# A block factorisation on one core: two units applied ahead instead of one, and part of the i·U halves made by a VectorE shuffle

## The reference, cut to what matters

```python
def cal_wfft_ortho(weight, n, cout, cin):
    vfft = jnp.fft.rfft2(weight, s=(n, n), norm='ortho')      # n = 34
    vfft = jnp.transpose(vfft, (2, 3, 0, 1))
    vH = jnp.conj(jnp.swapaxes(vfft, -1, -2))
    wfft = vH @ vfft                                          # 127 x 127 complex, per frequency
    ...
    wfft = wfft + eps[..., None, None] * jnp.eye(m)
    ortho = I - 2.0 * (vfft @ jnp.linalg.solve(wfft, vH))
xfft = rfft2(pad(groupnorm(x)));  zfft = ortho @ xfft
return x + irfft2(zfft)[crop] + bias
```

## Time and profile before

| | |
|---|---|
| median of three runs | 2853.52 us (2851.91 to 2857.53) |
| span of the profiled execution | 2851.4 us |
| outside the span, against the median | 2.1 us |
| PE / weight load / DVE busy | 2466.2 / 2018.1 / 1900.5 us |
| ACT / POOL busy | 1390.0 / 503.3 us |
| mean granted clock of PE | 0.928 |

### The profile page before, as it was taken

How to read it: one execution, slowest core, us unless ns; L and a number is a source line. 1 busy time by engine, 2 the same in 40 slices (tenths; PEclk the granted TensorE clock), 3 DMA queues, 4 the chain that set the end, 5 groups by cost and what they waited for, 6 DMA issues and landing times. The chain is left out here.

```text
span 2851.4 us, 89547 instructions
## 1 busy us (share of the span) xinstructions
PE 2466.2 (86%) x37953; PEld 2018.1 (71%) x37953; DVE 1900.5 (67%) x4779; ACT 1390.0 (49%) x3469; POOL 503.3 (18%) x872
## 2 busy tenths in 40 slices
PE   4975977999999899998987978787888888997999
PEld 4954744666566687777866767675776776987998
DVE  6852446888979768585768888897886885002444
ACT  1422422344353466665764646464565563772332
POOL 0002412121310011111111101010322221440000
PEclk7977988999999999999998989898899999997999
DMA  5274476331411283663835334361312323555874
GB/s 193 90 127 85 77 144 157 113 122 68 154 45 44 37 165 77 120 121 70 170 62 102 74 77 96 56 122 31 112 61 61 113 69 115 165 164 125 213 215 138
DMA packets 562604, 310.03 MB, mean 109 GB/s; under 512 B 484616, under 2 KB 495496, under 8 KB 561368
## 3 DMA queue, kind: packets, MB, share of 16 engines
q1 hardware_dynamic: 520896, 183.58, 30.7%
q0 software_dynamic: 41312, 120.73, 13.1%
HBM read 162.85 MB, written 141.30 MB: 107 GB/s over the span
## 5 line engine op out<-in xcount | busy, mean ns | idle before, releaser
L1499 DVE SCALAR_TENSOR_TENSOR arena<-arena,psum 128x512 f32<-128x512 f32 (+2 forms) x608 | 399.0, 720 | 322.5 <-PE psum L1063 322.4
L1063 PE MATMUL psum<-arena 32*128 32x128 f32 (+1 forms) x9280 | 300.4, 274 | 13.7 <-ACT arena L1250 9.7
L1040 PEld LDWEIGHTS psum<-arena 32*32 32x32 f32 x9280 | 162.0, 137 | 202.6 <-issue 201.1
L1063 PEld LDWEIGHTS psum<-arena 32*128 32x128 f32 x9280 | 279.0, 186 | 35.1 <-ACT arena L1250 20.3
L1002 PE MATMUL psum<-arena 128*32 128x256 f32 (+1 forms) x3696 | 262.7, 379 | 35.0 <-DMA arena<-plain 27.9
L1211 ACT COPY arena<-arena 32x128 f32<-32x128 f32 (+2 forms) x608 | 244.6, 402 | 92.4 <-DVE arena L1510 71.9
L1446 DVE TENSOR_TENSOR arena<-arena 128x320 f32<-128x320 f32 (+6 forms) x600 | 260.5, 485 | 8.2
L1040 PE MATMUL psum<-arena 32*32 32x64 f32 x9280 | 184.4, 231 | 89.2 <-DVEq L1491 78.7
L941 POOL COPY arena<-arena 128x512 f32<-128x512 f32 (+2 forms) x160 | 86.1, 584 | 830.1 <-ACT arena L1211 830.1
L1110 PE MATMUL psum<-arena 128*128 128x160 f32 x1160 | 198.8, 314 | 28.2 <-ACT arena L1290 28.1
L998 PE MATMUL psum<-arena 128*32 128x256 f32 (+1 forms) x2576 | 214.5, 401 | 9.9 <-DVE arena L1499 6.9
(11 more groups left out here) (126 smaller groups left out, 5020.6 us busy)
## 6 DMA issues: line engine op xcount, KB each, us to landing
blocks<-arena POOLq DMA_DIRECT2D x145, 256.0 KB, 2.3
arena<-blocks SPq DMA_DIRECT2D x290, 128.0 KB, 2.8
kept<-arena POOLq DMA_DIRECT2D x145, 256.0 KB, 3.1
arena<-kept SPq DMA_DIRECT2D x145, 256.0 KB, 3.0
xhat<-arena SPq DMA_DIRECT2D x32, 580.0 KB, 14.9
arena<-xhat SPq DMA_DIRECT2D x580, 32.0 KB, 2.6
yhat<-arena POOLq DMA_DIRECT2D x290, 64.0 KB, 2.5
arena<-x SPq DMA_DIRECT2D x8, 2048.0 KB, 9.8
```

The source lines that it names most:

```text
L1040: ins = pe.matmul(psum[0][h, L * t:L * t + L], ce[h, sj % NCE, :, slot + t], M[h, home(q) + t, c, :], start=True, stop=True)
L1063: ins = pe.matmul(upd_bank(u, c)[:, L * t:L * (t + m)].rearrange("p (a q m) -> p a q m", a=m, q=LB), rows.rearrange("p q r m -> p (q r m)" ...
L1499: ins = dve.scalar_tensor_tensor(old, old, K["mask"][:, piv:piv + 1], upd_bank(u, c)[:, 0:L * n].rearrange("p (t n) -> p t n", n=L), ALU.m ...
```

## The change

- Three unit buffers instead of two (`unit_slots`): one where the first was, two in the memory of `work`. `slot_of` deals them out in turn. ACT therefore waits, before the second and third unit of a sweep, for the stores that read `work` (`work_stored`), and the loads of form tables on SP wait for the sweeps before them.
- PE applies two units ahead: apply u+2, turn u+1 (where there is one), update u. A sweep starts with two applies.
- `PRODUCT_TURNS` names the units whose i·U is still made by `turn_u` and `copy_ju`: 0, 1, 2, 5, 8 of a sweep of a, and 2, 5 of one of b. For the others, 6 in a and 6 in b, 96 in all, ACT first writes U times a column of signs (`signed`, an activation with a scale from memory), and DVE exchanges the two halves of each 32 partitions by `stream_shuffle` into the odd half of the buffer. `ju_copied` and `ju_shuffled` count the two kinds (`turned_by`).
- On DVE the shuffle of unit u+2 stands ahead of the update of unit u; in a sweep of b those of the first two units stand ahead of everything.

```diff
+PRODUCT_TURNS = [(0, 1, 2, 5, 8), (2, 5)]
...
+        unit_slots = [Carve(at_)(8, LB, 2, B) for at_ in (EMB_AT, WORK_AT, WORK_AT + UW)]
+        signed = Carve(EMB_AT + UW)(2, UW // 2)
...
                     def turn_u(u):
                         q, n, p, sj = sweep_units[u]
                         pe.wait_ge(S["u_copied"], u + 1)
-                        if u:
-                            pe.wait_ge(S["ju_copied"], u)
+                        if turned_by[u] > 1:
+                            pe.wait_ge(S["ju_copied"], turned_by[u] - 1)
...
                     def update(u):
                         q, n, p, sj = sweep_units[u]
-                        pe.wait_ge(S["ju_copied"], u + 1)
+                        pe.wait_ge(S["u_copied"], u + 1)
+                        pe.wait_ge(S["ju_copied" if by_product[u] else "ju_shuffled"], turned_by[u])
                         if u:
                             pe.wait_ge(S["upd_copied"], 2 * u - 1)
...
                             apply(lo)
-                            turn_u(lo)
+                            apply(lo + 1)
+                            if by_product[lo]:
+                                turn_u(lo)
                             for u in range(lo, hi):
-                                if u + 1 < hi:
-                                    apply(u + 1)
+                                if u + 2 < hi:
+                                    apply(u + 2)
+                                if u + 1 < hi and by_product[u + 1]:
+                                    turn_u(u + 1)
                                 update(u)
-                                if u + 1 < hi:
-                                    turn_u(u + 1)
...
                     def copy_u(u):
...
+                        if not by_product[u]:
...
+                            act.activation(signed[:, u % 2, 0:L * n], psum[0][:, 0:L * n], ACT.Copy,
+                                           scale=K["sign"]).then_inc(S["u_signed"], 1)
+                        if used_before[u] >= 0:
+                            act.wait_ge(S["upd_done"], used_before[u] + 1)
...
+                    def shuffle(u):
+                        n = sweep_units[u][1]
+                        dve.wait_ge(S["u_signed"], turned_by[u])
+                        dve.stream_shuffle(unit_slots[slot_of[u]][:, 0:n].rearrange("p t q r m -> p (t q) r m")[:, :, 1, :],
+                                           signed[:, u % 2, 0:L * n].rearrange("p (a m) -> p a m", m=B),
+                                           [i ^ B for i in range(2 * B)]).then_inc(S["ju_shuffled"], 1)
...
+                        for u in range(lo, hi):
+                            if u + 2 < hi and not by_product[u + 2]:
+                                shuffle(u + 2)
                             update(u)
```

More of the change, by code:

```diff
@@ L190, in tables @@
     c["nturn"] = -turn
+    c["sign"] = np.where(ri == 0, 1.0, -1.0)[:, None]
     c["avg"] = (i[:, None] // 4 == i[None] // 4) / 4.0
@@ L777, in build @@
                 jobs.append((kind, g, k, at, len(where)))
+        slot_of, used_before, by_product, turned_by = {}, {}, {}, {}
+        for at_, (kind, g, k, lo, hi) in enumerate(jobs):
+            if kind == "sweep":
+                mids = [j[4] for j in jobs[:at_] if j[0] == "mid"]
+                turns = [0, 2, 1] if mids and mids[-1] % 2 else [0, 1, 2]
+                for u in range(lo, hi):
+                    slot = turns[(u - lo) % 3]
+                    used_before[u] = max([v for v in slot_of if slot_of[v] == slot], default=-1)
+                    slot_of[u], by_product[u] = slot, u - lo in PRODUCT_TURNS[g]
+                    turned_by[u] = 1 + sum(by_product[v] == by_product[u] for v in turned_by)
         def last_part(kind, g, k):
@@ L900, in _ @@
                                 sp.wait_ge(s_stored, 16 * NP * 2 * 2)
+                            if kind == "form" and before("sweep", at):
+                                sp.wait_ge(S["upd_done"], before("sweep", at))
                             for n, (of, _, first, _, _, _) in enumerate(loads):
@@ L1059, in update @@
                             for c in range(QUAD):
-                                rows = u_emb[quadrant(cls(p, c)), u % 2, t]
+                                rows = unit_slots[slot_of[u]][quadrant(cls(p, c)), t]
                                 m = 1 + (t < n - 1)
@@ L1239, in copy_u, with work_stored @@
                     def copy_u(u):
-                        q, n, p, sj = sweep_units[u]
+                        n = sweep_units[u][1]
                         act.wait_ge(S["u_done"], u + 1)
-                        if u >= 2:
-                            act.wait_ge(S["upd_done"], u - 1)
-                        act.copy(u_emb[:, u % 2, 0:n].rearrange("p t q r m -> p (t q) r m")[:, :, 0, :],
+                        if not by_product[u]:
+                            same = [v for v in range(u) if v % 2 == u % 2 and not by_product[v]]
+                            if same:
+                                act.wait_ge(S["ju_shuffled"], turned_by[same[-1]])
+                            act.activation(signed[:, u % 2, 0:L * n], psum[0][:, 0:L * n], ACT.Copy,
+                                           scale=K["sign"]).then_inc(S["u_signed"], 1)
+                        if used_before[u] >= 0:
+                            act.wait_ge(S["upd_done"], used_before[u] + 1)
+                        act.copy(unit_slots[slot_of[u]][:, 0:n].rearrange("p t q r m -> p (t q) r m")[:, :, 0, :],
                                  psum[0][:, 0:L * n].rearrange("p (a m) -> p a m", m=B)).then_inc(S["u_copied"], 1)
                     def copy_ju(u):
-                        q, n, p, sj = sweep_units[u]
-                        act.wait_ge(S["j_turned"], u + 1)
-                        act.copy(u_emb[:, u % 2, 0:n].rearrange("p t q r m -> p (t q) r m")[:, :, 1, :],
+                        n = sweep_units[u][1]
+                        act.wait_ge(S["j_turned"], turned_by[u])
+                        act.copy(unit_slots[slot_of[u]][:, 0:n].rearrange("p t q r m -> p (t q) r m")[:, :, 1, :],
                                  psum[1][:, 0:L * n].rearrange("p (a m) -> p a m", m=B)).then_inc(S["ju_copied"], 1)
+                    def work_stored(at, u):
+                        done = mid_quads[0:before("mid", at)]
+                        for n in range(2):
+                            if slot_of[u] == n + 1 and done[n:]:
+                                act.wait_ge(S[f"part_stored{n}"], 16 * len([q for q in done if q % 2 == n]))
+                            if slot_of[u] == 2 and before("final", at):
+                                act.wait_ge(S[f"y_stored{n}"], 32 * len(final_quads[n:before("final", at):2]))
                     def copy_blocks(m):
@@ L1344, in _ @@
                             copy_u(lo)
-                            copy_ju(lo)
+                            work_stored(at, lo + 1)
+                            copy_u(lo + 1)
+                            if by_product[lo]:
+                                copy_ju(lo)
                             pieces_of = pivots_beside(at)
                             for u in range(lo, hi):
-                                if u + 1 < hi:
-                                    copy_u(u + 1)
+                                if u + 2 < hi:
+                                    if u == lo:
+                                        work_stored(at, u + 2)
+                                    copy_u(u + 2)
+                                if u + 1 < hi and by_product[u + 1]:
                                     copy_ju(u + 1)
@@ L1526, in _ @@
                             place(set_job_at[g, k, GROUPS[g][t]], t)
-                        for u in range(*[job[3:5] for job in jobs if job[0:3] == ("sweep", g, k)][0]):
+                        lo, hi = [job[3:5] for job in jobs if job[0:3] == ("sweep", g, k)][0]
+                        for u in (lo, lo + 1):
+                            if not by_product[u]:
+                                shuffle(u)
+                        for u in range(lo, hi):
+                            if u + 2 < hi and not by_product[u + 2]:
+                                shuffle(u + 2)
                             update(u)
```

15 lines of the change are left out of this document (9 added, 6 removed).

## The result

| | before | changed |
|---|---|---|
| median of 20 runs each, us | 2857.22 (2840.64 to 2872.5) | 2880.05 (2862.49 to 2902.28) |
| changed / before | | 1.0089 [1.007, 1.0109] |
| span of the profiled execution, us | 2851.4 | 2860.7 |
| mean granted clock | 0.928 | 0.916 (0.901 to 0.916 in the timed runs) |

The account below looks back on a forecast made before the run. PE was taken to bound a steady sweep, at 4.09 us a unit. Gains of 14.0 in a, -1.8 in b and 4.6 in (b,3), together 16.8, took the span from 2851.4 to 2834.6, the median to about 2837; range 2822 to 2858.

Parts of the forecast that it names:

- The steady loop: Mid-sweep, PE update to DVE's first two operations and back: 3.63 us a shuffled unit, 4.10 a product one.
- The shuffle: On DVE, 96 shuffles of 0.75 us each, hidden because up to 0.86 costs nothing.
- The rival of the long shuffle: DVE's shuffle takes 1.3 us (2854, chance 0.06) or 1.6 us (2878, chance 0.06).
- ACT: Signed copy of 0.69 us on ACT adds nothing to the path; (b,3) gains 4.9 us from later gathers.
- The opening: Sweep start, before the first update: 2.1 us later in a, 2.2 in b, with nothing given back.
- The middle of b: First to last update in sweeps of b: two intervals of 4.10 and five of 3.63, 20.5 us gained in all.
- The end of a sweep and the clock: After a sweep's last update: change of 0, with gaps of 0.6 us not triggering the half clock.
- the clock rival: PE's idle gaps lower its clock, one 1.6 us stretch in each sweep, 26 us: 2863, chance 0.09.
- the opening rival: Added opening work at 1.2 GHz costs 4.0 us, not 2.1, in 11 sweeps: 2858, no change, chance 0.16.
- The case against the clock rival: In (b,3), a 9 us window with PE busy in 6.64 kept full clock; 3.03 of 3.63 is more.
- Waits for stores, the third buffer: Early units of a sweep wait for `work` stores, and form table loads for (a,2): nothing added.

Follow-up runs that it names:

- gaps and openings filled: Changed kernel plus PE products of constants, results unused, in waits before updates and behind opening applies that had nothing behind them: 2849.39 us, 0.9977 of before.
- two ahead alone: Changed kernel with every unit turned by product and no shuffles, keeping two applies ahead and three slots: 2883.19 us, 1.0093 of before.

## Why the prediction was wrong, step by step

**The steady loop: right.** 3.63 and 4.10 us, and 2.92 for units of 6 quads, stand in the trace nearly wherever the clock is full (the exceptions are below). The limit, DVE's first two operations to PE's next update, was read from one wait of the earlier trace rows.

**The shuffle: right in effect, size off.** 0.862 measured, 0.75 taken; the cover of 0.86 just held, and PE's steady interval didn't move. The loading of its permutation, allowed for with 0.1, shows as 0.01 to 0.02. The rival of the long shuffle is out: the kernel with gaps and openings filled keeps all of them at 0.9977.

**ACT: right.** 0.687, where 0.69 was forecast. (b,3) went from 41.47 to 39.28 although its opening grew by 3.6 us; between its updates it gained 5.8, where 4.9 and 1.95 were forecast, with a first update slowed by 0.97.

**The opening: right at full clock, wrong in what it costs.** (b,0) opens in 6.18 us, as forecast, though the terms written out for it add up to 6.03, not 6.2. Over the sixteen it cost 39.4 in place of 34.4, nearly all of the excess in a. In six sweeps of b the clock was at half for a part of the opening or the first update, in four before; (b,3) and (b,5) had none before. The forecast argued that the clock rises while the added work runs. In (b,5) it fell: apply, wait for two copies, apply leaves PE idle 1.4 of 2.5 us, and the slow part reaches into the first update (3.69 in place of 2.02). The kernel with two ahead alone shows the price of order and clock together: 27 us, of which filling gives 17 back.

**The middle of b: too much gained.** 12.6 in place of 20.5. The first interval is 4.68 to 8.17 instead of 4.10, 11.3 us too long over the eight. Of these 6.5 us are first updates that run at 1.2 GHz in part (2.61 to 3.69 us in six sweeps, 2.02 in the others); they weren't in the sum. The rest goes with PE standing for 0.34 us in (b,0) and (b,1), and 1.67 in (b,7), with nothing named that it waits for. With the first units turned by product all eight first updates take 2.02 and the interval is 4.11 or 4.12 in seven; with openings filled they take 2.02 too, and four intervals are 4.11 or 4.12.

**The end of a sweep and the clock: the step that failed.** The sum took the clock inside and outside the sweeps as it was, and put the end of a sweep at 0. Measured, half clock in the sweeps went from 78 to 147 us, and the ends of a cost 8.8. Where the windows were to shrink by 16.8 they grew by 9.5: of these 26, the ends of a make 8.8, the middle of b 7.9, the middle of a 5.1 (3.6 of it the slow interval before the last update in three sweeps) and the openings 5.0. I gave the clock rival 0.09 and a sum of 2863, the opening rival 0.16 and 2858. I weighed them as alternatives. They go together: two units ahead with products taken out leave PE idle in part, in the opening as in the tail, and in both the clock falls. It takes both halves of the change: with one ahead, or with all turns by product, no end of a is slow. Added, 2837 + 21 + 26 = 2884, beside 2880 measured; that the sum is so near is in part luck, since only 9.5 of the 23 us stand in the windows of the sweeps. The case against the clock rival was a window with PE busy in 6.64 of 9 us at full clock. It was one favourable row; the earlier trace rows showed the opposite, and the end of a sweep, where no apply is left to fill the gap (0.78, then 1.35 idle), wasn't worked out at all. The Trainium skill, "TensorE: Matmul & The Clock Gate", Part 1, whose table of the two states ties the half clock to idleness, gave 2837: the trace doesn't agree with that reading, since the clock fell to 0.50 in (a,1) with PE never idle over 1.35 us.

**Waits for stores, the third buffer: nothing, right.** The only wait of the signed copy or of `copy_u` for a store that the trace names is 1.8 us long, once; and the kernel with one ahead and three slots has shorter sweeps than before.

**What stays open.** Some intervals of PE are longer (4.4 to 5.3 where 3.63 or 4.10 is the rule, 8 and more in (b,7)), with PE waiting for nothing that the trace shows. They are in every kernel, 5.44 and 8.05 in (b,7) before. No run was made for it. Of the 23 us by which the medians differ, the windows of the sweeps make 9.5; the other 13 aren't in the first profile at all. They go with the clock: outside the sweeps some 374 us are at half clock where 334 were, and 320 with gaps and openings filled. What makes it fall there was not tested, nor why the inverse transforms start with 34 to 65 us at half clock on the same work.

## What to carry to other kernels

Taking work from a busy TensorE gains only what the next loop leaves, and may turn the rest into gaps that lower its clock: price every freed microsecond at both clock levels, and in openings and tails above all. Where a gap can't be used, a product of constants into a free bank is a cheap trial, and a good first experiment, since it tells clock from order. Looking further ahead costs its opening in every short loop; with eight units to a sweep, one ahead was better than two.

## What the runs showed that I had not expected

- A 128x512 shuffle of float32 within groups of 32 partitions takes 862 ns (the transpose of the same tile 712); an activation of 128x512 from PSUM with a scale from memory 687 ns, where the plain copy beside it takes 615 (602 before).
- In (a,1) the clock fell to 0.50 inside an idle stretch of 1.35 us, after 9.80 us in which PE was busy in 8.08. With one ahead it was still full after an idle stretch of 1.34 ahead of the last update of (a,1), with an apply within the 1.45 of idle before.
- Products whose result nobody reads made the kernel before quicker by 0.46%.
- The clock is low for different lengths of time in the same stretch of inverse transforms, with PE at work in all of it: 63.9 or 76.4 us for 498 weight loads, at a mean clock of 0.86 and 0.71.
